# One kernel for a four-block Flamingo stack: where the conv result is turned in an expert round

## The reference, cut to what matters

```python
x = x + jnp.tanh(g_xattn[0]) * retention(_layernorm(x), ctx_2048, ...)
x = x + jnp.tanh(g_ffn[0]) * ternary_mlp(_layernorm(x), ...)
x = x + jnp.tanh(g_xattn[1]) * long_conv(ctx_2048, ctx_2048, _layernorm(x), ssm_kernel, D, 8)
x = x + jnp.tanh(g_ffn[1]) * experts(_layernorm(x), ...)
```

```python
g = jnp.einsum('td,ndh->tnh', xf, Wgate) + bgate      # 6 routed experts of 256
u = jnp.einsum('td,ndh->tnh', xf, Wup) + bup
h = jax.nn.silu(g) * u
eo = jnp.einsum('tnh,nhd->tnd', h, Wdown) + bdown
routed_out = jnp.einsum('tnd,tn->td', eo, w)          # w: softmax weights, masked
share = jax.nn.silu(xf @ Ws_up + bs_up) @ Ws_down + bs_down
```

## Time and profile before

| | us |
|---|---|
| median of 3 runs | 2033.63 |
| the profiled execution | 2035.08 |
| its span, first to last instruction | 2033.3 |
| TensorE busy in the span | 1907.3 (94%), mean granted clock 0.974 |
| VectorE, ScalarE, GpSimd busy | 1492.6, 993.7, 1024.6 |
| the six additions of half 0 to x in rounds 1 to 6 | begin at 1047.73, 1211.24, 1375.02, 1538.53, 1702.05, 1865.58 |

### The profile page before, as it was taken

One profiled execution on the slowest core, in us unless ns is written; L12 is line 12 of the kernel. 1 busy time (PEld: TensorE's weight loads), 2 busy tenths in 40 slices (PEclk: granted clock), 3 DMA queues, 4 the chain that ended last, 5 costly groups with the idle time before them and its releaser, 6 DMA issues.

```text
span 2033.3 us, 27275 instructions
## 1 busy us (share of the span) xinstructions
PE 1907.3 (94%) x9892; PEld 1550.1 (76%) x9922; DVE 1492.6 (73%) x2233; ACT 993.7 (49%) x1420; POOL 1024.6 (50%) x790
## 2 busy tenths in 40 slices
PE   6999769999996669999999999999999999999997
PEld 5888756666652648888888887887887888888786
DVE  5877569888884867867876877876886886787422
ACT  4447557776764434345336336436435533533532
POOL 1110145444430856655655755756566665666454
PEclk9999889999999779999999999999999999999999
DMA  5866415566655203224234233342342432422431
GB/s 195 313 241 230 177 47 135 152 160 170 145 116 127 84 12 134 89 97 142 72 110 146 78 114 93 116 119 82 111 129 63 151 90 87 148 71 73 139 99 53
DMA packets 170113, 249.70 MB, mean 123 GB/s; under 512 B 91356, under 2 KB 92764, under 8 KB 163708
## 3 DMA queue, kind: packets, MB, share of 16 engines
q1 hardware_dynamic: 169692, 247.86, 39.7%
q10 hardware_dynamic: 288, 0.10, 0.0%
HBM read 193.13 MB, written 33.69 MB: 112 GB/s over the span
## 4 chain that ended last, share of the span: by engine, by line
PE 58%; DVE 4%; POOL 2%; issue 2%; ACT 1%; DMA 1%; ACTq 0%; POOLq 0%; DVEq 0%
PE e_ps_out L54 5%; PE e_ps_out L56 5%; PE e_ps_out L55 5%; PE e_ps_u L54 5%; PE e_ps_u L56 5%; PE e_ps_u L55 5%; PE e_ps_g L54 4%; PE e_ps_g L55 4%; PE e_ps_g L56 4%; PE e_ps_m L56 4%; PE e_ps_m L55 4%; PE e_ps_m L54 4%; DVE e_pstats L2266 1%; PE e_ps_m L2829 1%; PE e_ps_m L2784 1%
## 5 line engine op out<-in xcount | busy, mean ns | idle before, releaser
L1423 POOL TENSOR_TENSOR e_gu_lo<-e_gu_raw,e_gu_hi 128x1024 fp32r<-128x1024 f32 (+1 forms) x128 | 278.3, 2177 | 163.7 <-ACT e_gu_hi L1729 163.3
L2253 DVE TENSOR_REDUCE e_x3T<-e_zp 128x128 f32<-128x1024 f32 x124 | 257.4, 2076 | 1.2
L1428 POOL TENSOR_TENSOR e_dn_lo<-e_dn_raw,e_dn_hi 128x512 fp32r<-128x512 f32 x128 | 181.2, 1418 | 140.7 <-ACT e_dn_hi L1735 139.8
L54 PE MATMUL e_ps_u<-e_xn_hi,e_gu_hi 128*128 128x512 f32 x512 | 203.1, 397 | 8.4 <-DVE gate_held L2181 8.4
L2186 DVE TENSOR_TENSOR e_hd_lo<-gate_held,e_hd_hi 128x512 fp32r<-128x512 f32 x128 | 149.3, 1166 | 77.0 <-ACT e_hd_hi L1759 76.7
L54 PE MATMUL e_ps_out<-e_dn_hi,e_hd_hi 128*128 128x512 f32 x512 | 201.7, 394 | 0.0
L55 PE MATMUL e_ps_u<-e_xn_lo,e_gu_hi 128*128 128x512 f32 x512 | 199.9, 390 | 0.0
L56 PE MATMUL e_ps_u<-e_xn_hi,e_gu_lo 128*128 128x512 f32 x512 | 199.9, 390 | 0.0
L56 PE MATMUL e_ps_out<-e_dn_hi,e_hd_lo 128*128 128x512 f32 x512 | 199.5, 390 | 0.0
L55 PE MATMUL e_ps_out<-e_dn_lo,e_hd_hi 128*128 128x512 f32 x512 | 199.5, 390 | 0.0
L1435 POOL TENSOR_TENSOR gate_held<-e_sg,e_wb 128x512 f32<-128x512 f32 x96 | 136.3, 1420 | 109.7 <-ACT e_sg L1743 64.4
(11 more groups left out here) (321 smaller groups left out, 5003.5 us busy)
## 6 DMA issues: line engine op xcount, KB each, us to landing
e_gu_raw<-in_mgu SPq DMA_DIRECT2D x96, 512.0 KB, 3.8
e_dn_raw<-in_md SPq DMA_DIRECT2D x128, 256.0 KB, 3.3
e_wb<-wts SPq DMA_DIRECT2D x8, 1536.0 KB, 6.6
c<-in_ctxT SPq DMA_DIRECT2D x8, 1024.0 KB, 6.6
raw_w<-in_w1T SPq DMA_DIRECT2D x8, 1024.0 KB, 4.9
x_held<-in_w2T SPq DMA_DIRECT2D x8, 1024.0 KB, 7.4
gates<-gate_held SPq DMA_DIRECT2D x8, 1024.0 KB, 5.0
vals<-o SPq DMA_DIRECT2D x8, 1024.0 KB, 5.1
```

Source lines behind the costliest of these rows:

```text
L54: nc.tensor.matmul(out, w_hi, x_hi, start=first, stop=False, skip_group_check=skip)
L1423: nc.gpsimd.tensor_tensor(gu_lo[:, s % 2, a], gu_raw[:, s % 2, a], f32(gu_hi[:, s % 2, a]), ALU.subtract).then_inc(gulo_done, 1)
L1428: nc.gpsimd.tensor_tensor(dn_lo[:, s % 2], dn_raw[:, s % 2], f32(dn_hi[:, s % 2]), ALU.subtract).then_inc(dnlo_done, 1)
L2253: nc.vector.tensor_reduce(x3T[:, lb].rearrange("p (b n) -> p b n", b=B)[:, :, hh * CD:(hh + 1) * CD], zv(5, (1, 8), (21, 8)), AX.X, ALU.ad ...
```

## The change

Only the order is changed, on two engines, in rounds 1 to 6 (in round 7 there is no next group, so the moved calls do nothing). On TensorE both halves of the conv result are turned around gate(13): half 0 ahead of it, half 1 behind it and ahead of up(13), where half 1 stood between down(12) and up(14). On VectorE the addition and the statistics of half 1 move ahead of gated(13), and each half's shift moves behind the next product or cut: half 0's behind gated(13), half 1's ahead of gated(14) instead of behind it.

```diff
 # VectorE, rounds 2 to 7 (round 1 the same, written out)
             at(cut_hd, i, 12)
+            at(add_x3, i + 1, 1)
+            at(nat_stats, i + 1, 1)
+            at(gated, i, 13)
             at(nat_shift, i + 1, 0)
-            at(gated, i, 13)
             at(cut_t, i + 2, 0)
             at(cut_hd, i, 13)
-            at(add_x3, i + 1, 1)
-            at(nat_stats, i + 1, 1)
+            at(nat_shift, i + 1, 1)
             at(gated, i, 14)
-            at(nat_shift, i + 1, 1)
             at(norm_stats, i + 2)
 # TensorE, rounds 2 to 7 (round 1 the same)
             at(down, i, 11)
+            at(turn_x3, i + 1, 0)
             at(gate, i, 13)
-            at(turn_x3, i + 1, 0)
+            at(turn_x3, i + 1, 1)
             at(up, i, 13)
             at(gate, i, 14)
             at(down, i, 12)
-            at(turn_x3, i + 1, 1)
             at(up, i, 14)
```

More of the change, by code:

```diff
@@ L2578, in _ @@
         cut_hd(1, 12)
+        add_x3(2, 1)
+        nat_stats(2, 1)
+        gated(1, 13)
         nat_shift(2, 0)
-        gated(1, 13)
         cut_t(3, 0)
         cut_hd(1, 13)
-        add_x3(2, 1)
-        nat_stats(2, 1)
+        nat_shift(2, 1)
         gated(1, 14)
-        nat_shift(2, 1)
         norm_stats(3)
@@ L2995, in _ @@
         down(1, 11)
+        turn_x3(2, 0)
         gate(1, 13)
-        turn_x3(2, 0)
+        turn_x3(2, 1)
         up(1, 13)
@@ L3000, in _ @@
         down(1, 12)
-        turn_x3(2, 1)
         up(1, 14)
```

## The result

The changed kernel takes 2022.62 us (median of 4 runs, 2022.46 to 2024.71) against 2033.35 (4 runs, 2032.94 to 2035.59): the ratio is 0.9947, with a 95% interval of 0.993 to 0.9965. Run again beside two of the experiments it took 2024.68 against 2033.88, ratio 0.9954 (0.994 to 0.9969). The forecast was 2023.5, a ratio of 0.995, which lies in both intervals.

The account below looks back on a forecast made before the run. TensorE's stream was taken as the bound, with a gap at up(15) behind gated(14). Profiled 2035.08 us minus 10.1 is 2025.0; the median run lies 1.45 below the profiled one, so 2023.5 us was forecast, range 2021.8 to 2027.5.

Parts of the forecast that it names:

- The bound and the ceiling: TensorE's stream sets the time; closing the gap at up(15) gains at most 5 x 1.97 + 0.26 = 10.1 us.
- TensorE's order: TensorE's new starts from turn(0) to the turn of xn, which comes at 20.82 us instead of 22.81.
- the cover of gate(13): gate(13) between the turns hides the first addition; without it turn(1) would stand at 0.79 and wait 1.6 us.
- The port: VectorE's nat_shift(0) against GpSimd's cut of gu(15) at the shared SBUF port: 0.16 us if first, 2.35 if it meets the cut.
- The early case: nat_shift(0) goes at 8.4 us, takes 0.16, and ScalarE's normalization of the first half starts at 8.65; full gain.
- no value between: Whichever instruction is first at the port decides nat_shift(0)'s time: 0.16 us alone or 2.35 beside GpSimd's cut.
- The chain behind it: After the first half's normalization: silu(14) to 12.3 us, weigh(14) to 13.7, power(1) to 14.5, gated(14) 15.7 to 16.4.
- The port pair's part: Rival, chance 0.13: nat_shift(0) meets GpSimd's cut in all rounds, 0.4 us each in 6; gain 7.7, time 2025.9.
- the uncovered turn: Rival, chance 0.06: turn(0) waits for the last reduction into x3T; 2026.2 us if 1 us later, 2032.2 if 2.
- The slower one: Rival, slower at chance 0.03: nat_shift(1) waits for ScalarE and GpSimd, gated(14) ends past 19.8 us, up(15) starts later.
- the two meetings: Two more 2.35 us meetings with a cut ahead of gated(14) put up(15) at 23.0: 20 us lost, 2054.

## Why the prediction was right

- *The bound and the ceiling.* TensorE's stream sets the round, and the gap costs 1.97 us by starts, not the 1.67 that the waits list. Starts give 22.78 before (20.06 and the 2.72 of gate(13)) against 20.84, 1.95 a round in five rounds, and 0.26 in round 6: 10.0 us. The round is 161.58 long (161.67 in one of five), 161.55 were forecast.
- *TensorE's order.* The predicted starts (0.79, 3.61, 4.40, 7.22, 9.94, 12.66, 15.38, 18.10, 20.82) came as 0.79, 3.62, 4.41, 7.23, 9.95, 12.67, 15.39, 18.11, 20.84. Both turns found their data: the last reduction was over 0.8 us or more ahead of turn(0), and 0.59 in the tightest round of the changed kernel's second profile. With both turns together the cover of gate(13) shows its price, 1.72 us.
- *The port.* The early case was right, and the shift's start at 8.40 us exact, with GpSimd's cut at 8.62. Part of that is luck: the forecast had the power end between 8.0 and 8.4, priced at 1.06 us, while it took 0.73 and ended at 7.83; at 8.40 the shift goes straight behind gated(13), placed at 7.7 to 8.4 in the forecast. The lead of 0.22 us is thin: in the kernel with turn(0) alone the cut is 0.06 ahead and costs nearly the whole gain. The rule of the Trainium skill ("SBUF — State Buffer", section "SBUF: two separate sides", the first in place holds the port pair for its whole instruction) agrees with these rows: 0.15 or 0.16 us when the shift is first, and when it is second it lasts until GpSimd's cut is over, to within 0.05 us. How long that is depends on the cut: 2.35 or 2.14 us here, but 1.24 in another part of the kernel before (shift at 893.54, GpSimd's cut of 1.28 us at 893.48). So the prediction's "no value between" holds for this cut, not for the instruction.
- *The chain behind it* was a little too short in my sum: weigh(14) took 1.65 us and power(1) 1.14, beside VectorE's cut of hd(13), so shift(1) went at 15.11 and not by 14.5. up(14) is done at 15.6, so 0.5 us of slack hid the error.
- *The rivals.* The port pair's part and the uncovered turn did not come about. The slower one did not either; power(0) late shows that it names the right chain, and VectorE's half alone that the time follows gated(14) as it says. That the chain could grow by the two meetings that it priced at 20 us was not shown.
- *What it did not say* is that VectorE's half adds little to the gain: 8.2 of the 10 us (5 x 1.58 and 0.26 by starts) come with TensorE's half alone, and the same end is reached with one VectorE call, the cut of t, moved in the second half's stead. That call's 2.49 us of idleness was part of the chain in the trace, and my account of the cause named only the addition, the statistics and the cut of hd(13); the cut of t it mentioned as what round 6 lacks, without a price. Nor did it say that gated(13) ahead of the shift takes 0.57 us from the shift's lead over GpSimd's cut.

## What to carry to other kernels

When an in-order engine releases the bounding one too late, follow its own queue back to the first idle time and count every instruction from there: here two different edits of that chain closed the gap, two more left 0.26 and 0.36 us of it a round, and one half of a good edit alone cost 1.3%. Two instructions that must be first at a shared port are a race, and its winner can be read from the trace: 0.06 us decided it here. Of two orders with the same time take the one with the longer lead (0.79 against 0.22 us). Put a long independent block between two steps that hand a buffer back and forth.

## What was not expected of the hardware

A late release costs TensorE more than the idle time shown: the first block behind it takes 2.81 to 2.86 us instead of 2.72, and in round 6 before, in the late cut of t and in TensorE's half alone, about 0.26 to 0.36 us a round were lost without any wait in the list; with power(0) late and shift(1) behind gated(14) it was 0.60. The distance between the starts of blocks shows them, the waits don't.

A longer wait also costs clock: behind 3.97 us of idleness the granted clock fell to 0.50 and the next 12 matmuls took 4.42 to 5.26 us, while it stayed at 1.00 behind waits of 1.67 us.
